# A four-layer gated cross-attention block on one core: PE's bias work put behind the first keys and values, one load wait moved, mask loads last

## What is computed

```
x = x + tanh(g_xattn[0]) * xattn0(layernorm(x), ctx, ctx)
    query = z @ Wq + bq;  key = ctx @ Wk + bk;  value = ctx @ Wv + bv
    weights = softmax(where(mask == 0, -inf, query @ key.T / 16))
x = x + tanh(g_ffn[0]) * moe0(layernorm(x))    # 8 experts, each picks its top 256 of 2048 tokens, plus a shared MLP
x = x + ...  16-head attention, a linear map given in the frequency domain
x = x + ...  16-head attention, ternary MLP
x = x + ...  1-head attention, top-1 gated experts
```

## Time and profile before

| | us |
|---|---|
| median of 3 runs | 1067.26 (1066.99 to 1068.4) |
| the profiled execution | 1066.44 |
| its span, first to last instruction | 1064.7 |
| PE busy in the span | 880.7 (83%) |
| DVE, ACT, POOL busy | 445.1, 358.8, 201.0 |

### The profile page before, as it was taken

The page is one execution under the profiler, slowest core; times in us unless marked ns, Lnnn a source line. Parts: engine busy times, 40 slices in busy tenths (PEclk is TensorE's granted clock), DMA queues, the critical chain, the costliest instruction groups (busy, mean ns, idle before and its releaser), DMA issues. The chain is left out here.

```text
span 1064.7 us, 15292 instructions
## 1 busy us (share of the span) xinstructions
PE 880.7 (83%) x5758; PEld 662.4 (62%) x5758; DVE 445.1 (42%) x1209; ACT 358.8 (34%) x731; POOL 201.0 (19%) x202
## 2 busy tenths in 40 slices
PE   5888999998998968898776899874789797299996
PEld 4774666677877846665454566642457576288775
DVE  1675543301222146554274655524667477300000
ACT  1432222221222225554311455542668433022120
POOL 0127100012335200000010000001445313312122
PEclk9996999989999979999867999997889999599999
DMA  6033600017545280000000000000000001334351
GB/s 199 21 120 127 234 2 19 21 40 257 169 145 152 41 296 2 1 2 1 1 1 0 1 2 1 2 1 1 1 0 1 1 34 62 112 122 158 107 175 18
DMA packets 33870, 70.54 MB, mean 66 GB/s; under 512 B 9218, under 2 KB 23946, under 8 KB 28939
## 3 DMA queue, kind: packets, MB, share of 16 engines
q1 hardware_dynamic: 27081, 60.18, 15.8%
q0 software_dynamic: 6144, 8.31, 4.1%
q10 hardware_dynamic: 578, 1.13, 0.3%
HBM read 54.98 MB, written 14.80 MB: 66 GB/s over the span
## 5 line engine op out<-in xcount | busy, mean ns | idle before, releaser
L1201 ACT ACTIVATE arena<-banks 128x512 f32<-128x512 f32 (+4 forms) x159 | 92.3, 598 | 324.0 <-PE banks L902 64.6
L592 PE MATMUL banks<-arena 32*128 32x240 f32 (+6 forms) x1808 | 163.4, 380 | 19.2 <-DVE small L1883 14.8
L592 PE MATMUL banks<-ffw,arena 128*128 128x256 f32 (+2 forms) x640 | 126.4, 355 | 18.7 <-DVE x L1977 15.0
L592 PEld LDWEIGHTS banks<-arena 32*128 32x128 f32 (+5 forms) x1808 | 102.7, 165 | 53.1 <-issue 28.8
L592 PE MATMUL banks<-arena,ew 128*128 128x256 f32 x512 | 120.2, 395 | 7.9 <-ACT arena L1201 5.0
L592 PE MATMUL banks<-ew,arena 128*128 128x256 f32 x512 | 114.6, 382 | 8.8 <-ACT arena L1330 4.6
L592 PEld LDWEIGHTS banks<-ffw,arena 128*128 128x128 f16 (+1 forms) x640 | 86.8, 140 | 51.1 <-issue 20.5
L592 PEld LDWEIGHTS banks<-arena,ew 128*128 128x128 f32 x512 | 101.1, 199 | 24.7 <-ACT arena L1201 6.9
L592 PEld LDWEIGHTS banks<-ew,arena 128*128 128x128 f32 x512 | 96.0, 190 | 25.6 <-ACT arena L1332 6.8
L1883 DVE TENSOR_REDUCE small<-banks 128x16 f32<-128x1920 f32 x32 | 69.0, 2158 | 22.7 <-PE banks L592 22.3
L1381 ACT ACTIVATE arena<-banks,mcol 120x2048 f32<-120x2048 f32 x32 | 63.2, 1974 | 23.9 <-PE banks L592 23.9
(11 more groups left out here) (233 smaller groups left out, 1246.1 us busy)
## 6 DMA issues: line engine op xcount, KB each, us to landing
ew<-in_w SPq DMA_DIRECT2D x32, 1024.0 KB
xrow<-arena SPq DMA_DIRECT2D x1, 2064.0 KB, 21.0
arena<-xrow SPq DMA_DIRECT2D x8, 258.0 KB, 4.4
zrow<-arena SPq DMA_DIRECT2D x8, 256.0 KB, 2.2
ffw<-in_shared SPq DMA_DIRECT2D x2, 1024.0 KB, 6.1
acc<-x SPq DMA_DIRECT2D x4, 512.0 KB, 2.9
ffw<-in_tern SPq DMA_DIRECT2D x2, 1024.0 KB
out<-x SPq DMA_DIRECT2D x8, 256.0 KB
```

What stands on the lines that cost most here:

```text
L592: return pe.matmul(o, l, r, start=a, stop=b)
L1201: return nc.scalar.activation(o, i_, ACT.Copy)
```

## The change

In TensorE's order the bias columns go behind `turn_z(0)` and the key row behind `keys_values(1)`, so that `keys_values(0)` follows the product at once. ScalarE's `take_row` moves behind `take_z(0)`, to match. TensorE's wait for `ctx` moves ahead of `keys_values(0)`, and its wait for `base` moves to the first `logits`. In SyncE's order the last four `base` loads go ahead of the six mask loads. VectorE's and GpSimd's programs are not touched.

```diff
@@ SyncE
             sp.dma_start(bits[:, :, :], d["bits"]).then_inc(load["base"], 16)
+            sp.dma_start(tokt[:, :], d["tokt"]).then_inc(load["base"], 16)
+            sp.dma_start(iota16[:, :], d["iota16"]).then_inc(load["base"], 16)
+            sp.dma_start(b1T[:, :], d["b1T"]).then_inc(load["base"], 16)
+            sp.dma_start(lnwb[:, :, :], d["lnwb"]).then_inc(load["base"], 16)
             sp.dma_start(m1_8[0:NB, :], d["m1"].rearrange("o (b s) -> (o b) s", b=NB)).then_inc(load["masks"], 16)
...
             sp.dma_start(fsc[0:SK, :], d["fside"].rearrange("o (b s) -> s (o b)", b=NB), allow_slow_non_contiguous=True).then_inc(load["masks"], 16)
-            sp.dma_start(tokt[:, :], d["tokt"]).then_inc(load["base"], 16)
-            sp.dma_start(iota16[:, :], d["iota16"]).then_inc(load["base"], 16)
-            sp.dma_start(b1T[:, :], d["b1T"]).then_inc(load["base"], 16)
-            sp.dma_start(lnwb[:, :, :], d["lnwb"]).then_inc(load["base"], 16)
@@ TensorE
             product(psum[4], WT[:, 1], WT[:, 0]).then_inc(su["B_ps"], 1)
-            column(psum[5][:, 0:KC], WT[:, 0], COL["k0"])
-            column(psum[5][:, KC:2 * KC], WT[:, 1], COL["q0"])
...
-            pe.wait_ge(load["ctx"], 16)
-            pe.wait_ge(su["col_sb"], 1)
-            key_row(psum[6])
+            def bias_columns():
+                column(psum[5][:, 0:KC], WT[:, 0], COL["k0"])
+                column(psum[5][:, KC:2 * KC], WT[:, 1], COL["q0"])
...
+                m.then_inc(su["col_ps"], 1)
+            def first_key_row():
+                pe.wait_ge(su["col_sb"], 1)
+                key_row(psum[6])
...
                 def logits(k):
+                    if L == 0 and k == 0:
+                        pe.wait_ge(load["base"], 16 * 8)
                     pe.wait_ge(gt["zT_sb"], b0 + k + 1)
...
                 if L == 0:
+                    pe.wait_ge(load["ctx"], 16)
                     pe.wait_ge(load["values"], 32)
-                    pe.wait_ge(load["base"], 16 * 8)
                 keys_values(0)
                 for s in range(NB + 2):
                     if s < NB:
                         turn_z(s)
+                    if L == 0 and s == 0:
+                        bias_columns()
                     if 1 <= s <= NB:
                         turn_p(s - 1)
                     if s + 1 < NB:
                         keys_values(s + 1)
+                    if L == 0 and s == 0:
+                        first_key_row()
                     if s < NB:
                         scores(s)
@@ ScalarE
               .then_inc(su["B_sb"], 1)
-            take_row(psum[6], 1).then_inc(su["row_sb"], 1)
...
                     if s < NB:
                         take_z(s)
+                    if L == 0 and s == 0:
+                        take_row(psum[6], 1).then_inc(su["row_sb"], 1)
                     if 1 <= s <= NB:
                         take_p(s - 1)
```

More of the change, by code:

```diff
@@ L641, in _ @@
             product(psum[4], WT[:, 1], WT[:, 0]).then_inc(su["B_ps"], 1)
-            column(psum[5][:, 0:KC], WT[:, 0], COL["k0"])
-            column(psum[5][:, KC:2 * KC], WT[:, 1], COL["q0"])
[L644 to L647, removed]
-            pe.wait_ge(load["ctx"], 16)
-            pe.wait_ge(su["col_sb"], 1)
-            key_row(psum[6])
+            def bias_columns():
+                column(psum[5][:, 0:KC], WT[:, 0], COL["k0"])
+                column(psum[5][:, KC:2 * KC], WT[:, 1], COL["q0"])
+                for k in range(KC):
+                    m = mm(psum[5][0:1, 2 * KC:2 * KC + 1], cols[:, COL["q0"] + k:COL["q0"] + k + 1],
+                           cols[:, COL["k0"] + k:COL["k0"] + k + 1], k == 0, k == KC - 1)
+                m.then_inc(su["col_ps"], 1)
+            def first_key_row():
+                pe.wait_ge(su["col_sb"], 1)
+                key_row(psum[6])
             def one_gate(L):
```

## The result

| | before | changed |
|---|---|---|
| median of 22 runs each, us | 1067.76 (1065.57 to 1072.84) | 1070.27 (1068.35 to 1073.09) |
| the profiled execution | 1066.44 | 1071.06 |
| its span | 1064.7 | 1069.2 |
| mean granted clock of the span | 0.928 | 0.922 |

The ratio is 1.0022, with a 95% interval of 1.0013 to 1.0031: slower by 2.5 us, by about the 0.2% that the text before took as the bound. The forecast was 1066.6. The time lies inside the range, in its upper end, where the first rival was.

A forecast was written before the change was run, and what follows sets the result against it. PE's wait for `lnwb` before its first keys was taken as the bound. The reordered front steps summed to 0.6 us earlier: 1067.26 - 0.6 = 1066.66, say 1066.6, range 1063.9 to 1071.0.

The forecast's parts named there:

- the first rival: Front stage: PE's lower clock level stays through the bias columns; +3.2 to +6.2 us, near 1072; chance 0.2.
- The steps of the sum: Front stage's PE work added up: first scores at 27.85 against 28.73, second batch's normalised x 0.6 us earlier.
- keys and values: First keys and values start at 15.78 instead of 22.84 and take 3.54 us, to 19.32.
- turned x: PE's turn behind the first keys and values: 0.7 us, between 0.50 quick and 0.91 slow.
- bias columns: Now on the path behind turned x: 2.1 us, against 3.58 at the slow pace.
- second keys and values: Behind the bias columns: 1.85 us, to 23.95.
- key row: Behind the second keys and values: 1.0 us, between 0.9 and 1.78, to 24.95.
- the uncovered chain: ScalarE's copy and VectorE's add of the key row before the first scores: 2.85 us, PE idle.
- The edits put at nothing: Moved ctx and base waits, reordered base and mask loads, and ScalarE's take_row: no cost expected.
- the part on the clock: PE's pace: the sum assumes the rise to 2.4 GHz at about 19.7, after the first keys and values, and lasting.
- milder form: Clock falls during PE's new idle time of 25 to 27.8 us; no size of its own given.
- The second rival: Clock rises by 15.8, so first keys and values need 1.85 us; 2.8 us earlier, 1064.5; chance 0.13.

The follow-up runs named there:

- e9_wait_only: Kernel before with one edit, the wait for the eight base loads moved to the first logits; 1064.47 against 1068.14, ratio 0.9960.
- e10_before_warm: Kernel before, load wait in place, plus 18 dummy matmuls before the weights land; 1068.04 against 1068.14, ratio 0.9997.
- e2_masks_back: Changed kernel with SyncE's loads back in the order of before; 1067.21 against 1064.97 for the kernel before, ratio 1.0016.
- r_after: Changed kernel run once more, nothing altered; 1067.42 against 1064.40 for the kernel before, ratio 1.0030.
- e3_filled: Changed kernel plus five dummy matmuls behind the key row, in the idle stretch; 1064.77 against 1064.97 for the kernel before, ratio 0.9994.
- e4_row_first: Changed kernel with the key row ahead of the second keys and values; 1063.56 against 1064.97 for the kernel before, ratio 0.9986.
- e7_after_warm: Changed kernel plus 18 dummy matmuls before the weights land; 1066.97 against 1068.14 for the kernel before, ratio 0.9990.
- e8_row_behind: e1_old_order with the key row alone moved behind the second keys and values; 1070.28 against 1068.14 for the kernel before, ratio 1.0012.
- e5_filled_both: Changed kernel plus six dummy matmuls before the first scores and two behind them; 1063.83 against 1064.40 for the kernel before, ratio 0.9988.
- e1_old_order: Kernel before with the base wait at the first logits and mask loads last, PE and ACT order kept; 1059.36 against 1064.97, ratio 0.9940.
- r_before: Kernel before run once more for its trace, nothing altered; one run, 1064.06.
- e6_warm: e1_old_order plus 18 dummy matmuls before the weights land; 1056.20 against 1064.40 for the kernel before, ratio 0.9923.

## Why the prediction was wrong

**What bounds the front stage: right.** The wait for `lnwb` was the last to end; one edit that takes it away wins 0.4% (e9_wait_only), and no gain ahead of it arrives (e10_before_warm).

**The steps of the sum: right in their sizes.** Counted from the start of the first keys (15.78 forecast, 16.37 measured, for the weights that landed 0.59 later): keys and values 3.56 against 3.54, turned x 0.85 against 0.7, bias columns 1.94 against 2.1, second keys and values 1.95 against 1.85, key row 0.99 against 1.0, the uncovered chain 3.02 against 2.9. First scores at 16.37 + 12.31 = 28.68, where the sum gave 12.07 for the same stretch. The edits put at nothing cost nothing that shows: the loads (e2_masks_back against the changed kernel), the logits, which waited 0.20 us and not for a load, and the masks. `lnwb` landed at 21.3 (issued at 9.78, 11.5 us to landing), not near 20; so the new order of loads alone, with the wait in its old place, would have freed no more than about 1.5 us (an estimate from 22.84 and 21.3).

**The step that failed** is the assumption in the part on the clock, "that the rise comes at about 19.7, at the end of the first keys and values, and lasts". It came, at 20.8, and did not last. It fell at 27.6, in the wait of 3.02 us that the sum had priced by its length alone. From the start of the first scores to the second turned x it then took 4.27 instead of 2.89 us, the turns behind them 1.33 instead of 0.72, and the keys and values of the next round 3.54 instead of 1.84: 3.7 us in all. The first scores themselves came at 28.68 against 28.73, where 0.88 earlier was forecast; 0.6 of that gain went to the late weights. So the front was 3.6 us late and not 0.6 early, and PE's clock, which the sum had at nothing behind 19.7, is the term.

**The first rival, half right.** Its mechanism, the lower level through all the bias columns, did not come: in the three traces the clock rose at 19.6, 20.8 and 21.4, at most 0.7 us behind the start of the columns, and they took 1.94 to 2.31 us and not 3.58. What came was its "milder form", the fall in the new idle time, which I had named and not priced; r_after had, besides, a fall 1.1 us behind the columns that no rival named. The three traces lie 3.3 to 8.3 us behind before at 64 us, and the profiled execution's 1071.06 lies near the 1072 of this rival. I gave this rival 0.2 where all eight traces with either move had a fall by 31 us. That its number fits is partly luck, since its sum got there by slow columns, keys and key row.

**The second rival's condition came too, and did not help.** In six traces PE's program is the same up to the bias columns, and its clock rose at 14.4, 15.3, 19.6, 20.0, 20.8 and 21.4 us (first turns at 8.6 to 9.3). Twice, in e3_filled and e4_row_first, that is before 15.8, and the first keys and values took 1.86 us. The fall behind the columns or in the waits came all the same. So the sentence that the product "had not raised" the clock holds for the trace of before and not for each execution.

**What I overlooked in the rows** is how far the order of before was already favourable for the clock. There the sparse work lay where PE was slow anyway, and the dense work came in one piece from 22.84 on, with the key row's chain beside it. The change put the sparse work and the idle time where PE was quick. The sum counted both as time alone. The Trainium skill's page "TensorE: Matmul & The Clock Gate", section "HAM oscillation — how this bites in real kernels", describes a clock that falls in PE's gaps and is slow for the work behind, with waits for DMA as the cause of the gaps. The traces of the changed kernel, e2_masks_back, e7_after_warm and e8_row_behind agree: a wait of 3.02 us, here for ScalarE and VectorE, and the fall in it or at most 1.6 us behind it. In r_after, e4_row_first and e5_filled_both the clock fell first at 23.0, 22.1 and 23.4 us, where PE had had no wait longer than 0.7 us since the product; what came ahead there is the columns, and that section does not describe this. The page's remark in "The HAM clock gate" that the monitor runs free of the kernel's start agrees with the six rises of one order of work, which lie 7.0 us apart where the first turns lie 0.6 apart.

**The large rest.** By medians e1_old_order is 5.6 us faster, where its front is 2.0 ahead. The sitting of e1_old_order has no trace of before; r_before is of another, with nearly the same median of before. It had a fall at 74.9, in the scores, that neither e1_old_order nor the first trace of before had:

```profile
75.00:78.30 3.30, 3.30 (x14) 3.03 (x14) 1.52 (x6) 0.48 (x3) 0.55 (x1) 0.50 0.26 84
```

There it lost 1.3 us. The profiled executions of the two kernels lie 3.2 us apart (1060.82 and 1064.06), about what front (2.1) and fall (1.3) make; the other 2.4 us lie between them and the medians (that of e1_old_order is the slowest of its six). That the rest comes from later falls of the clock is only argued, from one trace of each kernel; it stays open.

## What to carry to other kernels

In this kernel the sparse TensorE work (bias columns, single rows) was best placed where TensorE was slow anyway, and the chain over two other engines beside dense matmuls. When work is moved to fill a wait, ask what TensorE does in the stretch where the work lands and just behind it: an idle stretch of 3 us there cost 3 us once, and as much and more again through the clock. First try the smaller edit: here the wait moved by itself was worth 0.4%, and the reordering around it took all of it back.

## What the runs showed beyond this

- Dummy matmuls from 2.8 to 9 us, while the weights load, make the front stage 3.2 us shorter than in e1_old_order (differences to the first trace of before of -5.2 against -2.0 us at 64 us), a fall at 34.9 us included. With a load wait behind them they gained nothing (e10_before_warm), and in the changed order 0.1% (e7_after_warm), with an interval that reaches no change.
- A fall of the clock before 31 us was followed by another one 17 to 21 us later in e2_masks_back, e8_row_behind and e5_filled_both; the first two were 8.3 and 7.5 us behind at 55 us. But e9_wait_only and e6_warm fell at 40.0 and 34.9 without one ahead, at the turns and values of an early batch, so the order of before is not safe from falls in the loop either; each cost 2.9 us.
- One stage, from 893 to 930 us in the first trace of before, where the top-1 gate's rows are moved by DMA, goes by the sitting and not by the kernel. It takes 36.8 to 37.4 us in six traces (before, changed, and the four of the third sitting) and 33.7 to 34.1 in the eight of the first two. These 3 us are about what the medians of before differ by: 1067.76 and 1068.14 against 1064.97 and 1064.40. Without the kernel before in the same sitting, a change of 0.3% cannot be read.
